# Second attention of a graph transformer: keys-values in the queries' banks, four units behind them, stacked query squares, and key features rounded by GpSimd

## What is computed

```python
def _phi(t, random_features):
    norm_sq = 0.5 * jnp.sum(t * t, axis=-1, keepdims=True)
    proj = jnp.einsum('bhnd,md->bhnm', t, random_features)
    return jnp.exp(proj - norm_sq) * (1.0 / math.sqrt(M))
...
q_p = _phi(q, random_features)
k_p = _phi(k, random_features)
kv = jnp.einsum('bhnm,bhnd->bhmd', k_p, v)
out = jnp.einsum('bhnm,bhmd->bhnd', q_p, kv)
k_sum = jnp.sum(k_p, axis=2)
normalizer = jnp.einsum('bhnm,bhm->bhn', q_p, k_sum)[..., None]
out = out / (normalizer + 1e-06)
```

## Time and profile before

| | |
|---|---|
| Median of 3 runs | 1966.47 us (1963.76 to 1967.13) |
| The profiled execution | 1964.45 us, of it the span 1962.7 us |
| Mean granted TensorE clock | 0.992 of full |
| PE busy in the span | 1874.1 us (95%) |
| DVE / ACT / POOL busy | 1206.3 / 873.1 / 94.3 us |
| Second attention, pairs 0 to 5 | from 987.7 us to 1150.8 us after the span's start |

### The profile page before, as it was taken

The page is one execution under the profiler, slowest core; times in us unless marked ns, Lnnn a source line. Parts: engine busy times, 40 slices in busy tenths (PEclk is TensorE's granted clock), DMA queues, the critical chain, the costliest instruction groups (busy, mean ns, idle before and its releaser), DMA issues. The chain is left out here.

```text
span 1962.7 us, 32306 instructions
## 1 busy us (share of the span) xinstructions
PE 1874.1 (95%) x13051; PEld 1767.6 (90%) x13051; DVE 1206.3 (61%) x1909; ACT 873.1 (44%) x1176; POOL 94.3 (5%) x84
## 2 busy tenths in 40 slices
PE   5899899999999999998999999899999999999999
PEld 4899789999999999998899989798878888888899
DVE  8467786444343345446557777675666668899732
ACT  6456521222211212224477762423655557777620
POOL 0000000000000000000010100100111101100000
PEclk9999999999999999999999999899999999999999
DMA  3311235121111112110211041424877779999831
GB/s 92 98 46 36 63 106 122 57 60 54 57 57 57 52 52 78 49 49 17 89 33 34 17 153 41 161 77 176 287 237 242 216 228 335 366 380 374 295 119 40
DMA packets 157962, 250.53 MB, mean 128 GB/s; under 512 B 11949, under 2 KB 86189, under 8 KB 157460
## 3 DMA queue, kind: packets, MB, share of 16 engines
q1 hardware_dynamic: 152532, 231.21, 35.6%
q0 software_dynamic: 5040, 17.56, 3.7%
q10 hardware_dynamic: 272, 0.07, 0.0%
HBM read 228.80 MB, written 20.01 MB: 127 GB/s over the span
## 5 line engine op out<-in xcount | busy, mean ns | idle before, releaser
L183 PE MATMUL psum<-products_room 128*128 128x512 f32 (+2 forms) x2160 | 457.1, 366 | 3.1 <-DVE re_credit L3735 2.0
L183 PEld LDWEIGHTS psum<-products_room 128*128 128x128 f32 (+1 forms) x2160 | 388.4, 187 | 47.1 <-issue 2.3
L183 PE MATMUL psum<-ring_hi,xt_sb 128*128 128x256 f32 (+3 forms) x1920 | 355.5, 283 | 9.7 <-PEq L1292 2.8
L3632 DVE TENSOR_TENSOR products_room<-moe_raw,products_room 128x1536 fp32r<-128x1536 f32 x179 | 312.5, 1755 | 76.7 <-ACT products_room L3531 74.1
L3531 ACT ACTIVATE products_room<-moe_raw 128x1536 fp32r<-128x1536 f32 x179 | 266.0, 1489 | 151.8 <-PE psum L183 81.0
L183 PEld LDWEIGHTS psum<-ring_hi,xt_sb 128*128 128x128 f32 (+1 forms) x1920 | 299.8, 188 | 11.4 <-issue 6.3
L183 PE MATMUL psum<-ring_lo,xt_sb 128*128 128x256 f32 (+3 forms) x960 | 270.5, 282 | 0.0
L183 PEld LDWEIGHTS psum<-ring_lo,xt_sb 128*128 128x128 f32 (+1 forms) x960 | 180.5, 188 | 0.0
L183 PE MATMUL psum<-ring_hi,gnn_sb 128*128 128x256 f32 (+1 forms) x810 | 147.8, 283 | 5.0 <-DVE gnn_sb L1192 3.6
L139 DVE TENSOR_TENSOR ring_lo<-ring_raw,ring_hi 128x1536 fp32r<-128x1536 f32 (+1 forms) x64 | 119.4, 1866 | 50.5 <-ACT ring_hi L128 50.5
L191 PE MATMUL psum<-xt_sb,ring_hi 128*128 128x314 f32 x744 | 139.9, 310 | 0.3
(11 more groups left out here) (532 smaller groups left out, 2746.2 us busy)
## 6 DMA issues: line engine op xcount, KB each, us to landing
moe_raw<-in_L_ffn_Wg_r SPq DMA_DIRECT2D x60, 768.0 KB, 6.3
moe_raw<-in_L_ffn_Wu_r SPq DMA_DIRECT2D x60, 768.0 KB, 6.3
moe_raw<-in_L_ffn_Wd_r SPq DMA_DIRECT2D x60, 768.0 KB, 9.3
ring_raw<-in_L_gnn_w_rel SPq DMA_DIRECT2D x18, 896.0 KB, 5.2
ring_raw<-in_L_mix_W_qkv SPq DMA_DIRECT2D x24, 384.0 KB, 4.2
ring_raw<-in_L_gnn_w_rel SPq DMA_DIRECT2D x9, 768.0 KB, 4.6
ring_raw<-in_L_gnn_w_root SPq DMA_DIRECT2D x6, 896.0 KB, 5.1
count_total_dram<-gnn_sb POOLq DMA_DIRECT2D x3, 1570.0 KB, 11.6
```

Of the source, the lines that this page charges most:

```text
L183: mm = pe.matmul(out, lhs[a], rhs[b], start=(first and i == 0), stop=(last and i == 2))
L3632: dve.tensor_tensor(wlo[:, i % RING, :], raw[i % RAWS], whi[:, i % RING, :].bitcast(F32), ALU.subtract)\
```

## The change

Six edits, all for the second attention:

1. The squares of the queries are stacked. ScalarE writes the rounded squares of each head into its own 64 rows of a plane of its own (two instructions of 64 rows, where there was one of 128), GpSimd the low part of the same head into the other 64 rows (two of 64 rows where there was one of 128). One matmul with `minus_half` (all 128 rows -0.5) then does what two did.
2. GpSimd makes the rounded copy of the key features (`key_features_high`), five per pair, where ScalarE did. TensorE's second part of the query features now waits for `pk_f` and not `pk_hi`.
3. `keys_values` writes to bank pair 0, where query parts 0 and 2 are made, and waits for `pq_hi` of part 2. The wait of the next pair's unit 0 for `kv_f` is gone.
4. Of the six query units, one stands behind part 0, one behind part 3, and four behind `keys_values`.
5. Four lead units in banks 2 to 5, in 24 steps of three matmuls (`lead_steps`), laid between the parts of the last pair.
6. ScalarE makes the next pair's key squares behind part 3 of the query features, not part 0.

```diff
+LEAD_BANK, LEAD_UNITS = 2, 4
...
-            nh = k.sb(f"{name}_nh", [P, 512], F32R)
+            nh = k.sb(f"{name}_nh", [P, 2], F32R)
+            minus_half = k.sb(f"{name}_minus_half", [P, P], F32R)
...
-            return k.pair[1][:, hd, 0:2 * VW].rearrange("p (e v) -> p e v", v=VW)
+            return k.pair[0][:, hd, 0:2 * VW].rearrange("p (e v) -> p e v", v=VW)
...
-            def square_low(p):
-                for a in (KEYS, QUERIES):
...
+            def key_square_low(p):
+                pool.wait_ge(s["sq_hi"], qk_count(p, KEYS))
...
+            def query_square_low(p):
+                pool.wait_ge(s["sq_hi"], qk_count(p, QUERIES))
+                if p >= 1:
+                    pool.wait_ge(s["pq_mm"], 4 * p)
+                pool.wait_ge(s["sq_lo"], qk_count(p, KEYS))
+                for hd in range(2):
+                    if hd == 1:
+                        pool.wait_ge(s["sq_half"], p + 1)
+                    ins = pool.tensor_tensor(sq[other(hd), QUERIES, hd, :], sqf[own(hd), QUERIES, :],
+                                             sq[own(hd), QUERIES, hd, :].bitcast(F32), ALU.subtract)
+                    ins.then_inc(s["sq_half"] if hd == 0 else s["sq_lo"], 1)
+                pool.wait_ge(s["sq_lo"], qk_count(p, QUERIES))
+
+            def key_features_high(p):
+                for t in range(TT):
+                    pool.wait_ge(s["pk_f"], p * TT + t + 1)
+                    if p >= 1 and t == 0:
+                        pool.wait_ge(s["kv_mm"], p)
+                    pool.tensor_copy(phik[0:TS[t], t, 0, :], pf[0:TS[t], t % 2, 0:512]).then_inc(s["pk_hi"], 1)
 
             if second:
+                key_square_low(0)
+                query_square_low(0)
                 for p in range(PAIRS):
-                    square_low(p)
+                    key_features_high(p)
+                    if p + 1 < PAIRS:
+                        key_square_low(p + 1)
+                        query_square_low(p + 1)
...
-                        pe.wait_ge(s["pk_hi"] if second else s["pk_lo"], TT * (p + 1))
+                        pe.wait_ge(s["pk_f"] if second else s["pk_lo"], TT * (p + 1))
...
-                        for a in range(2):
-                            for h in range(2):
-                                mm = pe.matmul(pair[:, h, 0:HN], nh[:, m * P:(m + 1) * P],
-                                               sq[:, QUERIES, a, h * HN:(h + 1) * HN], start=False, stop=(a == 1))
+                        for h in range(2):
+                            mm = pe.matmul(pair[:, h, 0:HN], minus_half[:], sq[:, QUERIES, hd, h * HN:(h + 1) * HN],
+                                           start=False, stop=True)
...
-                    if second and p == PAIRS - 1 and m == 1:
-                        lead_unit(0)
-                    if second and m < 3:
-                        project_unit(p + 1, KD + m)
+                    if second and m != 1 and m != 2:
+                        project_unit(p + 1, KD + m // 3)
+                        if p == PAIRS - 1:
+                            lead_steps(2 * KD + m, 2 * KD + m + 3)
...
-                    pe.wait_ge(s["sq_hi"] if second else s["qk_lo"], qk_count(p + 1, KEYS))
...
+                if second:
+                    pe.wait_ge(s["pq_hi"], 4 * p + 3)
...
-                    for u in range(KD + 3, 2 * KD):
+                    for u in range(KD + 2, 2 * KD):
...
+                for hd in range(2):
+                    ins = act.activation(halves(sq[own(hd), a, hd, :]), qk_pair[a][own(hd), :, 0:HN], ACT.Square)
+                ins.then_inc(s["sq_hi"], 1)
...
-                        act.wait_ge(s["pk_f"], i + 1)
-                        act.activation(phik[0:TS[t], t, 0, :], pf[0:TS[t], t % 2, 0:512], ACT.Copy).then_inc(s["pk_hi"], 1)
...
-                    if m == 0 and p + 1 < PAIRS and second:
+                    if m == 3 and p + 1 < PAIRS and second:
                         squares(p + 1, KEYS)
...
-TURN_BANK = (6, 2, 4, 0, 6)
+TURN_BANK = (6, 0, 2, 4, 6)
...
-FIRST_BANK = 4
-LEAD_UNITS = 2
+FIRST_BANK = LEAD_BANK

```

More of the change, by code:

```diff
@@ L390, in project_unit @@
                     pe.wait_ge(*st.split(n))
-                    if p >= 2 and second:
-                        pe.wait_ge(s["kv_f"], p - 1)
-                    elif p >= 2:
+                    if p >= 2 and not second:
                         pe.wait_ge(s["num_f"], 2 * (p - 2) + 1)
@@ L431, in features_k @@
                     project_unit(p + 1, t)
+                    if second and p == PAIRS - 1:
+                        lead_steps(2 * t, 2 * t + 2)
                 project_unit(p + 1, TT)
+                if second and p == PAIRS - 1:
+                    lead_steps(2 * TT, 2 * KD)
             def features_q(p):
@@ L459, in features_q, with lead_steps @@
                             pe.wait_ge(s["sq_lo"], qk_count(p, QUERIES))
-                        for a in range(2):
-                            for h in range(2):
-                                mm = pe.matmul(pair[:, h, 0:HN], nh[:, m * P:(m + 1) * P],
-                                               sq[:, QUERIES, a, h * HN:(h + 1) * HN], start=False, stop=(a == 1))
+                        for h in range(2):
+                            mm = pe.matmul(pair[:, h, 0:HN], minus_half[:], sq[:, QUERIES, hd, h * HN:(h + 1) * HN],
+                                           start=False, stop=True)
                     mm.then_inc(s["pq_mm"], 1)
-                    if second and p == PAIRS - 1 and m == 1:
-                        lead_unit(0)
-                    if second and m < 3:
-                        project_unit(p + 1, KD + m)
-                    elif m == 1:
+                    if second and m != 1 and m != 2:
+                        project_unit(p + 1, KD + m // 3)
+                        if p == PAIRS - 1:
+                            lead_steps(2 * KD + m, 2 * KD + m + 3)
+                    elif m == 1 and not second:
                         for u in range(KD, KD + 3):
                             project_unit(p + 1, u)
-            def lead_unit(u):
-                if u == 0:
-                    pe.wait_ge(*st.next.split(0))
-                    pe.wait_ge(s["qk_lo"], qk_count(PAIRS - 1, QUERIES))
-                    pe.wait_ge(s["sq_lo"], qk_count(PAIRS - 1, QUERIES))
-                wh = st.next.views(0)
-                for j in range(KD):
-                    split_product(pe, k.banks[4 + u][0:TS[u], 0:256],
+            def lead_steps(n0, n1):
+                wh = st.next.views(0)
+                for n in range(n0, n1):
+                    u, j = divmod(n, KD)
+                    if n == 0:
+                        pe.wait_ge(*st.next.split(0))
+                    split_product(pe, k.banks[LEAD_BANK + u][0:TS[u], 0:256],
                                   [k.xt[:, j, a, u * P:u * P + TS[u]] for a in range(2)],
@@ L635, in _ @@
                     act.wait_ge(s["pk_mm"], i + 1)
-                    if p >= 1 and t == 0:
-                        act.wait_ge(s["kv_mm"], p if second else 2 * p)
+                    if p >= 1 and t == 0 and not second:
+                        act.wait_ge(s["kv_mm"], 2 * p)
                     if second:
```

32 lines of the change are left out of this document (16 added, 16 removed).

## The result

The changed kernel takes 1983.24 us in the median of four runs (1981.89 to 1985.08), the kernel before 1966.8 us on the same chip (four runs, 1963.76 to 1970.41). The ratio is 1.0081, 95% interval 1.0068 to 1.0095: **slower by 16.4 us**. Forecast were 1976.5 us (1964 to 1989) and slower with 0.75.

What follows compares the result with a forecast made beforehand. The prediction took TensorE to bound the middle pairs. Four middle pairs +8.0, pair 0 -1.2, last pair +3.3, next phase 0 gave +10.1 on 1964.45 us; with 2.0 from execution to median, 1976.5 us, range 1964 to 1989.

Steps and rivals of the forecast that it cites:

- eight matmuls: TensorE, every pair: the stacked query squares remove eight matmuls, -1.17 us a pair.
- tile 4: Key tile 4, middle pairs: TensorE waits 2.1 us for two GpSimd subtractions, cast, VectorE low part and ScalarE exponential in turn.
- query parts 2 and 3: Middle pairs: late exponentials and missing units make TensorE wait 1.4 us before part 2, 0.3 before part 3, together 1.75.
- `attend`: Middle pairs: the old wait for keys-values' low part vanishes, -0.74 us counted from issue to issue.
- gone in pairs 0 to 4: Wait before `attend`: the fourth unit behind keys-values adds 0.88 us of work and covers the 0.57 us wait.
- The two prices of GpSimd: On GpSimd: a 64-row subtraction costs 1.54 us (lower bound 0.77), a 512-element cast 0.67 us (0.56 to 1.29).
- the rival of quick subtractions: On GpSimd: 64-row subtractions take half, 0.77 us; total +2 to +4 us, 1968.5 to 1970.5 us; chance 0.13.
- Pair 0: First pair: query squares are made early, so only 0.7 us of waits at query parts 2 and 3 show; -1.2 us.
- The last pair: Old waits go (-4.5 us), matmuls go (-1.17), twelve more lead steps (+4.25) and new waits come; sum +3.3 us.
- The clock rival: TensorE's clock falls after each new wait, 1.5 us more a middle pair; +17 us, 1983.5 us; chance 0.06.
- The next phase paid nothing back: Phase after the pairs: two units (4.25 us) less work, but TensorE just waits longer, so its length changes by 0.
- the chain given for it: Next phase: reciprocal, load of `x`, element work and VectorE's chunk split end TensorE's wait 29.8 us after its start.

Runs made afterwards that it cites:

- Run 5: The changed kernel with ScalarE's squares of the next pair's keys back behind query part 0: 1985.95 us.
- Run 11: The changed kernel with query squares between the two denominators and VectorE's weight-chunk split moved behind keys-values and the next queries' low parts: 1973.76 us.
- run 6: The changed kernel with one query unit behind each of query parts 0 to 2 and three behind keys-values, as before the change: 1983.84 us.
- Run 4: The changed kernel with two lead units instead of four, in the same banks: 1982.33 us.
- run 7: The changed kernel with ScalarE's squares of the next pair's queries made between the two denominators, not behind both: 1973.82 us.
- run 3: The changed kernel with GpSimd's order changed: casts 0 and 1, first query-square subtraction, cast 2, second subtraction, casts 3 and 4, key squares: 1980.39 us.
- run 2: The changed kernel with the query squares in one GpSimd subtraction of 128 rows and four matmuls a part again, casts still on GpSimd: 1969.7 us.
- run 8: The changed kernel with query squares between the denominators and one 128-row subtraction with its matmuls back, casts still on GpSimd: 1966.68 us.
- run 10: The changed kernel with query squares between the denominators, one 128-row subtraction with its matmuls back, and rounded key copies on ScalarE: 1969.01 us.
- Run 9: The changed kernel with query squares between the denominators and the rounded key copies back on ScalarE: 1968.04 us.
- run 1: The changed kernel with the rounded key copies back on ScalarE, so that GpSimd does subtractions only: 1973.47 us.
- run 12: The changed kernel with key copies on ScalarE, query squares between the denominators, and VectorE's weight-chunk split behind keys-values: 1979.43 us.

## Why the prediction was right, and which of its sizes were off

**Right:** the direction, the place and the chain of the main wait. By the steps of the prediction, for pair 2 (all from issue to issue; a unit or part that does not wait starts 0.30 us behind the last pair of matmuls):

| term | forecast | measured | how |
|---|---|---|---|
| eight matmuls | -1.17 | -1.17 | subtracting the squares takes 0.29 us a part (1056.57 to 1056.86), 0.59 before; four parts make -1.2 |
| tile 4 | +2.1 | +2.28 | 1053.68 - 1051.10 - 0.30 |
| query parts 2 and 3 | +1.75 | +1.50 | 1.09 and 0.19 ahead of them, 0.22 because the first four matmuls of each take 0.69 (1059.71 to 1060.40) and not 0.58 |
| `attend` | -0.74 | -0.06 | 1071.39 - 1070.41 - 0.30 = 0.68 now, 0.74 before |
| small gaps at tile 2 | 0 | +0.22 | 0.12 and 0.10 |
| sum | +1.94 | +2.77 | pair: 30.28 - 27.39 = +2.89 |

- **The failed step is "gone in pairs 0 to 4"**, the wait in front of `attend`. It went in pair 0 and stayed in pairs 1 to 4. The unit put behind keys-values does stand there (0.88 us), but VectorE comes to keys-values later by nearly as much (6.30 us after TensorE's first matmul of it in pair 2, before 5.49). The key squares, moved behind query part 3 by edit 6, now meet VectorE's low parts, which cost 1143 ns each where they cost 874, and the 1.75 us of splitting stand behind them as before. Run 5 (squares early) takes the wait away by taking the new cause away. Run 11 (split late) takes it away by clearing VectorE's way; the split stood there in the kernel before as well. The prediction priced edit 6 at nothing and looked only at ScalarE. 0.68 us in four pairs is 2.7 us of the 7.3 by which the span grew more than the sum of the forecast (17.4 for 10.1).
- **The two prices of GpSimd were near.** 64 rows cost 1533 ns (forecast 1.54 us), so the rival of quick subtractions falls. A cast that begins while VectorE is idle takes 0.61 us (the first two of each of pairs 1 to 5, 609 to 614 ns; forecast 0.67, bounds 0.56 and 1.29). The 0.67 us at 1055.28 overlap the end of a low part (1054.79 to 1055.48), and a cast that starts together with a low part takes 1.06. The Trainium skill (GPSIMD Engine Reference, 3.1 Elementwise) would give an estimate of 0.61 with the fixed part of the earlier trace rows; the trace agrees. For two inputs that section has 2.6 cycles an element, where the prediction wrote 2.5; no sum rests on it.
- **Pair 0** came out at -0.9 for -1.2. The sum took away 0.74 us in front of `attend`, the wait of the middle pairs; in pair 0 it had been 0.20 us (0.37 from issue to issue), so half of the term was never there. The waits at the two parts were 0.34 and 0.20 us, for 0.7. **The last pair** at +3.5 for +3.3, but by terms that cancel: waits of 0.28, 2.44 and 0.49 us are less than the 4.7 forecast, and a stretch of lower clock, about 0.7 us by difference, makes up the most of it. That the sum came out is luck in part.
- **The clock rival came true in part.** Pairs 1 to 3 waited 2.08 to 2.12 us at tile 4 and kept their clock. Pair 4 waited 2.12 us too and is 0.7 us longer. Its loss was larger: from key tile 4 to query part 2 it takes 6.73 us with 0.19 of waiting, pair 2 6.03 with 0.95, so that the lower clock costs TensorE 1.5 us, of which 0.8 vanish in the later wait. Windows of the changed kernel, behind the wait in pair 2, around the one in pair 4, and in the last pair:

```profile
1055.00:1057.00 2.00, 2.00 (x15) 2.00 (x15) 2.00 (x3) 1.63 (x4) 1.20 (x2) 1.00 0.00 0
1112.00:1114.00 2.00, 0.08 (x1) 0.00 (x0) 1.85 (x2) 0.69 (x2) 0.67 (x2) 1.00 0.00 0
1114.00:1116.00 2.00, 1.80 (x8) 1.80 (x9) 1.50 (x4) 0.99 (x3) 1.26 (x2) 0.52 0.00 0
1116.00:1118.00 2.00, 2.00 (x11) 2.00 (x11) 1.59 (x3) 0.84 (x2) 1.48 (x2) 0.63 0.00 0
1146.00:1148.00 2.00, 2.00 (x11) 2.00 (x11) 1.73 (x3) 1.54 (x4) 0.94 (x3) 0.50 0.00 0
```

  The prediction's argument, that waits of this size are not enough, holds for three of the four here and for none of the four in run 6. The forecast should have carried a part of this rival (1.4 us in the two pairs).
- **The next phase paid nothing back**, as forecast: 93.20 us for 92.42. Run 4 says the same from the other side: two units fewer in the last pair cost nothing there (92.15 us). But the chain given for it is not what bound TensorE in this profile. The split of the chunk is done at 1195.75, 28.4 us after the first product, and TensorE comes to the matmul behind it at 1198.05, 30.7 us after, and does not wait; before it waited there until 29.8 us. The 4.25 us saved went on the way: in waits for the split of chunk 1 (1.08 us) and for a bank (2.97 us), both named in the prediction, and in a lower clock behind the second, which it did not have:

```profile
1176.17 0.58 PE L183 MATMUL psum<-ring_hi,xt_sb 128*128 128x256 f32 x1 [2.97 <-DVE p_graph L2730]
1198.05 0.28 PE L183 MATMUL psum<-ring_hi,p_at 128*128 128x256 f32 x1
```

```profile
1175.50:1182.30 6.80, 6.13 (x28) 6.13 (x29) 6.76 (x13) 1.33 (x3) 0.00 (x0) 0.50 0.83 267
```

  In runs 4 and 7, where the clock keeps its full level in this stretch, TensorE does wait for the split (1.39 and 1.33 us), and the wait ends 29.5 and 29.4 us after the first product. There the chain forecast sets the time; here the result agrees with it by luck in part.
- **Missed:** +0.5 us ahead of pair 0, where TensorE now waits 1.66 us for VectorE's low part of a value tile (`m_v`). Ahead of it VectorE splits a weight chunk, which takes 3.03 us for 1.76 because GpSimd's second subtraction for pair 0 (until 984.03) meets it:

```profile
982.61 3.03 DVE L139 TENSOR_TENSOR ring_lo<-ring_raw,ring_hi 128x1536 fp32r<-128x1536 f32 x1 [0.95 <-ACT ring_hi L128]
```

  In run 3 the two subtractions stand elsewhere; the split takes 1.76 us and the wait is 0.39. With one subtraction (runs 2, 8 and 10) there is none.
- The sum: four middle pairs +2.8, +2.9, +2.8 and +3.6, pair 0 -0.9, last pair +3.5, make 14.7. With 0.5 ahead, 0.8 in the next phase and 1.4 in the rest of the program, whose place is open, the span is 17.4 us longer.

**Where the gain went.** TensorE has 1.17 us less to do in a pair, and that never shows. Run 9 keeps the stack and the new places of the units, and GpSimd delays no key tile in it. Its pair is 27.56 us, that of run 10 without the stack 27.57, that of the kernel before 27.40: what the stack saves comes back as waiting at the query parts and at `attend`. To keep it, one would have to fill part 2 and `attend` both, with the six query units that there are; this is argued, no run did it. No version here beats the kernel before. Left untried is the split behind the copies of the attention results, and not ahead of them, which by the rows of run 11 could avoid the 1.67 us; what it makes late next is open.

## What to carry to other kernels

When work is moved to an idle engine, write down that engine's order and look at the first operation that another engine waits for: GpSimd was busy 5% of the time, and 3.15 us ahead of one cast of 0.61 cost TensorE 2.3 us a pair. Halving an operation's rows did not shorten it on GpSimd (1533 ns for 1546), so a form that trades one operation of 128 rows for two of 64 doubles it. For every step that is moved later, check which operation of VectorE it will now meet when it is GpSimd's, and remember that two edits on one chain do not add: starting that chain 1.7 us earlier was worth as much (9.4 us) as taking five operations out of it (9.8). Last, a wait that stays when its cause is removed may have got a second cause: look at what its releaser did just before, as at query part 2 in run 1.

## What the runs showed of the hardware

- GpSimd and VectorE both get longer when they meet in SBUF: a subtraction of 1.54 us took 2.08, two low parts of 1.53 took 2.87, a weight split of 1.76 took 3.03, a cast of 0.61 took 1.06, and a low part of 0.69 took 1.06. All these operations of VectorE have two inputs in SBUF. Beside a reciprocal, which has one (run 11, 1051.50), a cast kept its 0.61. The Trainium skill (SBUF — State Buffer, SBUF: two separate sides) calls the port pair that the two share an exclusive lock: a VectorE operation with two SBUF inputs and a GpSimd operation that reads SBUF exclude each other for a whole instruction. The rows fit it, if the waiting for the lock is counted as busy time in the profile: 1.06 is more than 0.69 by less than a whole cast.
- The same wait of TensorE can cost its length or that and 0.7 to 1.5 us more. Behind 2.12 us in three pairs the granted clock stayed at 1.00 (2.4 GHz), in the fourth it fell to 0.52, the lower level (1.2 GHz) in nearly all of the window. Behind the same 2.12 us in run 6 it fell in all four middle pairs, behind 1.67 us in run 11 in two pairs of five, in run 12 in three. What tells the two apart is not settled by these runs.
